# TensorE takes the turn and the routing of a step before the placing of the step ahead of it, in the third front of a transformer block

## The reference

```python
x = x + 0.5 * ffn(layernorm(x))          # 16 experts, two of them per token, and a shared expert
x = x + attention_and_moe(layernorm(x))  # linear attention, then 8 experts, two per token
x = x + 0.5 * ffn(layernorm(x))          # the first line again
```

```python
logits = jnp.einsum('btc,ec->bte', x, router_w)
top_vals, top_idx = jax.lax.top_k(logits, TOP_K)
gates = jax.nn.sigmoid(top_vals)
...
sg = jnp.einsum('btc,sc->bts', x, shared_gate_w)
su = jnp.einsum('btc,sc->bts', x, shared_up_w)
```

## Time and profile before

| | us |
|---|---|
| median of 3 runs | 840.58 (837.47 to 845.62) |
| the profiled execution | 843.14 |
| its span, first to last instruction | 841.4 |
| front3, from the first load of pairs to the first load of ffn3 | 539.17 to 664.22 |
| POOL busy over the span | 414.9 (49%) |
| PE busy over the span | 556.7 (66%) |
| granted TensorE clock, mean of the span | 0.808 |

### The profile page before, as it was taken

How to read it: one execution, slowest core, us unless ns; L and a number is a source line. 1 busy time by engine, 2 the same in 40 slices (tenths; PEclk the granted TensorE clock), 3 DMA queues, 4 the chain that set the end, 5 groups by cost and what they waited for, 6 DMA issues and landing times. The chain is left out here.

```text
span 841.4 us, 10790 instructions
## 1 busy us (share of the span) xinstructions
PE 556.7 (66%) x2860; PEld 414.7 (49%) x2860; DVE 385.1 (46%) x1192; ACT 282.3 (34%) x713; POOL 414.9 (49%) x444
## 2 busy tenths in 40 slices
PE   4897877883357879982396977337667187787720
PEld 3644766661235658761274755223223175676610
DVE  5781334331457669738311211278643044343327
ACT  5653333331143576631131313033434032232210
POOL 5217556544776551100466663247776045645540
PEclk9999899997567889965599897755767598989865
DMA  7151355441111110242111110242111222222228
GB/s 209 52 165 45 105 135 139 117 132 53 41 45 41 38 39 26 63 126 62 28 44 48 40 46 28 75 135 73 47 46 54 66 80 74 80 67 80 69 73 259
DMA packets 88518, 66.12 MB, mean 79 GB/s; under 512 B 10150, under 2 KB 80939, under 8 KB 88460
## 3 DMA queue, kind: packets, MB, share of 16 engines
q1 hardware_dynamic: 75596, 40.85, 17.1%
q0 software_dynamic: 11712, 24.04, 10.0%
q10 hardware_dynamic: 1152, 0.53, 0.2%
HBM read 36.63 MB, written 28.75 MB: 78 GB/s over the span
## 5 line engine op out<-in xcount | busy, mean ns | idle before, releaser
L1899 POOL DMA_INDIRECT ffn_pairs<-ffn_out,ffn_target x79 | 78.2, 990 | 81.1 <-ACT ffn_out L1980 42.5
L795 POOL DMA_INDIRECT ffn_rows<-norm_rows,core_gather_id x79 | 75.7, 958 | 58.7 <-issue 18.6
L299 POOL DMA_INDIRECT attn_back<-ffn_out_rows,core_back_slot x64 | 63.0, 984 | 34.3 <-issue 18.4
L1652 POOL DMA_INDIRECT expert_rows<-front_norm,front_slot_int x64 | 62.3, 973 | 27.9 <-issue 18.2
L1927 PE MATMUL ffn_gu_ps<-core_gate_up,ffn_rows_t 128*128 x158 | 50.4, 447 | 13.4 <-issue 8.3
L1481 POOL DMA_INDIRECT moe_pairs<-moe_out,core_scatter_id x40 | 39.4, 985 | 39.3 <-DVE moe_out L1566 29.5
L824 PE MATMUL ffn_gu_ps<-core_gate_up,ffn_rows_t 128*128 x158 | 46.2, 416 | 18.6 <-issue 11.1
L1542 ACT ACTIVATE moe_hid<-moe_hid_ps,core_b 128x320 f32<-128x320 f32 x64 | 31.7, 529 | 76.1 <-PE moe_hid_ps L1515 37.1
L893 DVE TENSOR_TENSOR ffn_hid<-ffn_gate,ffn_gu_ps 128x256 f32<-128x256 f32 (+1 forms) x40 | 16.7, 418 | 86.2 <-issue 63.2
L1992 DVE TENSOR_TENSOR ffn_hid<-ffn_gate,ffn_gu_ps 128x256 f32<-128x256 f32 (+1 forms) x40 | 16.7, 417 | 85.5 <-ACT ffn_gate L1973 50.3
L1515 PE MATMUL moe_hid_ps<-moe_rows_t,core_moe_w 128*128 128x320 f32 x128 | 42.5, 485 | 19.2 <-ACT moe_hid L1542 18.5
(11 more groups left out here) (275 smaller groups left out, 1353.7 us busy)
## 6 DMA issues: line engine op xcount, KB each, us to landing
ffn_rows<-expert_rows SPq DMA_DIRECT2D x79, 64.5 KB
ffn_out_rows<-ffn_out SPq DMA_DIRECT2D x39, 128.0 KB
core_moe_w<-in_w SPq DMA_DIRECT2D x8, 512.0 KB
moe_pairs<-core_zero SPq DMA_DIRECT2D x4, 1024.0 KB
front_pair<-moe_pairs SPq DMA_DIRECT2D x8, 512.0 KB, 5.0
last_pair<-ffn_pairs SPq DMA_DIRECT2D x8, 512.0 KB, 5.9
core_x<-in_x SPq DMA_DIRECT2D x8, 256.0 KB, 4.8
norm_rows<-front_norm SPq DMA_DIRECT2D x8, 256.0 KB, 2.2
```

Source lines behind the costliest of these rows:

```text
L299: pool.indirect_dma_start(out=self.got[j % self.depth][:, k, b, :], out_offset=None, in_=self.rows, in_offset=bass.IndirectOffsetOnAxis(ap ...
L795: pool.indirect_dma_start(out=rows[i % ring][:, h, :], out_offset=None, in_=core.norm_rows, in_offset=bass.IndirectOffsetOnAxis(ap=core.ga ...
L1652: pool.indirect_dma_start(out=core.expert_rows, out_offset=bass.IndirectOffsetOnAxis(ap=slot_int[:, j, g:g + 1], axis=0), in_=norm[j % rin ...
L1899: pool.indirect_dma_start(out=core.ffn_pairs, out_offset=bass.IndirectOffsetOnAxis(ap=target[:, n:n + 1], axis=0), in_=out[q % deep][:, h, ...
```

## The change

Only PE's loop in `front_scatter` is edited. `place` moves one turn of the loop down, with its argument lowered by one: in turn i PE now does the turn and the routing of step i, a unit, and then the placing of step i-1. The placing of step 7 falls into turn 8, between the units 12 and 13, and the totals follow in that turn too. No instruction is added or removed, and the queues of the other engines are the same row by row.

```diff
@@ -1831,11 +1831,11 @@
                 lo, hi = units_at(i)
                 if hi > lo:
                     units.product(nc, pe, core, lo, 0)
-                if i < S:
-                    place(i)
+                if 1 <= i <= S:
+                    place(i - 1)
                 for n in range(lo + 1, hi):
                     units.product(nc, pe, core, n, 0)
-                if i == S - 1:
+                if i == S:
                     pe.wait_ge(place_read, S)
```

## The result

The changed kernel took **869.98 us** (median of 4 runs, 863.90 to 872.23), the kernel before 841.04 (4 runs, 837.47 to 845.62). The ratio is 1.033, 95% interval 1.0255 to 1.0404: 3.3% slower, where 858.5 was forecast and 867 was the end of the range. The profiled execution took 872.23 us against 843.14, so 29.1 us are to be found. The mean granted clock is 0.805, against 0.808. Ratios leave out executions that count as disturbed by a slower state of the chip, on this one core by their time alone; none fell out here, but 6 of 12 did for the first kernel of experiment 5.

The account below looks back on a forecast made before the run. POOL was taken to set the pace at 11.54 us per step; a closed loop of 16.2 us per step, with start, table load and end, gave +17.9 us on the median of 840.58: 858.5 us, range 848 to 867.

Parts of the forecast that it names:

- case A: front3: the loop through POOL, ACT, PE and DVE closes with PE mostly slow, +13.7 to +21.1 us; chance 0.70.
- L: Chain from one step's first scatter to the next's in front3, taken as 16.2 us against POOL's 11.54 us.
- The walk: Sum of the chain's links in front3: 16.72 us per step with PE at 1.2 GHz, 13.99 at 2.4 GHz.
- table load: ACT's table load in step 3, between normalise and copy, now lies in the chain once: +1.28 us.
- End: End of front3: blanks 20.5 us behind placing 6, scatters last at 21.5, then 2.84 us to the next phase's load.
- bounds of 1 to 5 us: End of front3: bounds on the 2.84 us to the next load, as no row gave a scatter's landing time.
- Rival D: front3: late waits each count in the chain, or blanks or landing are slower; +27 to +30 us, chance 0.12.
- the one wait of POOL that the change was to remove: POOL's 3.87 us wait ahead of step 7 for slots, forecast to be gone in the new order.
- the upper bound of the gain: Earlier logits can only pay where POOL waits, ahead of step 7: at most 3.87 us.
- Rival C: front3: POOL stays the bound at 11.54 us per step, not slower; -2.6 us, 838, chance 0.06.
- The start: Start of front3: placing 0 waits for turn 1 and routing 1, at 559.30 in place of 558.05, +1.25 us.
- placing 7: Behind units 11 and 12, up to 7.04 us, covered by POOL's 9.80 us of scatters in step 6.

Follow-up runs that it names:

- experiment 5: Kernel before with blank tiles split SP 6, ACT 5, POOL 5: ratio 0.9984; first kernel, also with PE's placing ahead of the routing: ratio 0.9945.
- experiments 1: Changed kernel with the placing of step i-1 moved ahead of the shared expert's unit: 839.96 us, ratio 1.0073 to the kernel before.
- experiment 3: POOL's scaling of step j+2 moved behind all eight scatters of step j: changed kernel 889.43 us, ratio 1.0696; kernel before 833.43 us, ratio 1.0007.
- experiment 4: Changed kernel with POOL waiting for all 16 blank tiles ahead of step 7's scatters: 859.69 us in one run, 1.032 to the kernel before.
- experiment 2: Changed kernel with PE's order turn, placing of the preceding step, routing, unit, unit: 832.95 us, ratio 1.0022 to the kernel before.

## Why the prediction was right and where it failed

**Right: the loop and its price.** The mechanism of case A came out link by link, in the pace (experiments 1 and 3 move it by 3.6 and 5.2 us, where the links say 3.6 and 5.1), in the waits (the reader of the placing, L1754, waits 50.4 us in eight times, longest 8.9) and in what did not matter: the waits for logits in DVE's choice, up to 8.26 us in the earlier trace rows, are down to one of 2.1 us, and that bought nothing.

**Right in kind, short in size: L.** The walk gave 16.72 us with PE at 1.2 GHz and 13.99 at 2.4 GHz, and I took 16.2. The steps without the table load measured 16.58 to 16.76, since PE ran the head of every step at 1.2 GHz: the six together are +2.2 us over the forecast. (The walk itself was 0.14 us long, most of it in its first link, 6.34 for 6.15.) The 28% of fast clock that the earlier trace rows shows is there after too (0.65 over the six steps). But it falls behind the links of the chain: the unit behind the placing had a second product of 1.02 or 1.07 us in each step. All PE links of the chain stand ahead of that, right behind an idle stretch of 6.6 to 9.3 us in the steps 2 to 7, 7.12 in the rows shown. I had mixed a mean clock into a path on which only the slow part lies. The Trainium skill (TensorE: Matmul & The Clock Gate, section HAM oscillation — how this bites in real kernels) has the array cold again at each burst behind such a stretch; the trace agrees in each of these steps, with turns of 1.11 or 1.12 us and routings of 1.89, and the 16.72 that I set beside it was 0.14 off.

**Failed: the step "End".** There I let the blanks end 12.1 + 8.4 us behind placing 6, one microsecond ahead of the scatters, and gave the scatters 2.84 us to the next load. The 12.1 was right: 673.60 - 661.74 is 11.86. The 8.4 was wrong: beside scatters the eight issues took 16.74 us. In the kernel before ACT's blanks began at 653.00, after the last scatter's end at 652.36, so the earlier trace rows gave their price with POOL at rest. In the new order they begin 9.7 us ahead of that end. The tail became 10.60 us instead of 2.84, **+7.8 us**. That is the main miss. The sign that I passed over lay in the same trace, in the timeline of SP: its eight blanks, begun while POOL still scattered, took 11.34 us, though the last four of them, behind the last scatter, lie 1.09 us apart.

```profile
646.14 11.34 SPq L1626 DMA_DIRECT2D expert_rows<-front_blank  x8
```

The bounds of 1 to 5 us were set on the landing of a scatter, and experiment 4 puts that at 2.57; they were set on the wrong thing.

**Rival D.** It named the size (27 to 30 us) and, in its last sentence, blanks slower than I take them. But its main mechanism, late waits in the chain, did not occur: in the loop of the changed kernel ACT has no wait put down to "remote", where before it had five of 2.3 to 4.6 us, 16.2 together. In the tail came one such wait, DVE's of 8.85 us, beside ACT's slow issues. So that D's number fits is in part luck.

Those waits most likely explain the one wait of POOL that the change was to remove, too. ACT's timeline, kernel before, copies of the logits of steps 6 and 7:

```profile
623.21 0.22 ACT L1692 ACTIVATE front_logits<-front_logits_ps 128x64 f32<-128x64 f32 x1 [4.59 <-remote]
...
636.86 0.22 ACT L1692 ACTIVATE front_logits<-front_logits_ps 128x64 f32<-128x64 f32 x1 [3.18 <-remote]
```

The routings before them had ended at 620.04 and 634.28, so the copies came 3.2 and 2.6 us late, together more than 3.87. And in the profiled executions of experiment 3 (kernel before) and of experiment 5 (split alone) ACT has no such wait ahead of step 7, and that wait of POOL is absent. So the 3.87 us were a trait of some executions, and the upper bound of the gain was less firm than one row made it look.

**Rival C.** POOL's occupancy, the figure by which the Trainium skill (Perfetto Trace Analysis, section Identifying the Most-Contended Engine) picks what to work on, was 54.62 us of work before and 54.33 after in six steps; the time grew by 31 all the same. Experiment 3 says it more sharply.

**The rest.** The start was 1.53 for 1.25, the table load about 1.0 for 1.28, placing 7 was covered as said; 1.5 us of the profiled difference lie ahead of front3, where nothing was edited. From 17.9 the terms lead to 28.2: +7.8 for the tail, +2.2 for the pace, +0.3 for the start.

## What to carry to other kernels

When an instruction moves behind another on an engine that takes its work in order, walk once around every loop that this closes and compare its length with the busiest engine's step: up to that length the move is free (experiment 2), beyond it each microsecond counts once per step. On the loop use the durations of the place where each link will stand: here the matmuls behind PE's idle stretches of 6.6 to 9.3 us all cost their slow price, while the mean granted clock was 0.65. And before a transfer's or an issue's price is carried to a new place, look at what the other queues did while it was measured.

## What was not expected of the hardware

Beside POOL's indirect DMAs the queues of other engines can be held. Instructions with a median of 29 ns took up to 1409 ns, ACT's eight issues 15.5 to 16.7 us in place of 8.1 to 8.4, and ACT and DVE show waits of 2 to 9 us (once 13.8) whose releaser the trace calls "remote". In the stretches of this kind that were read, the DMA engines were busy for only 14 to 29% of the time.

Scatters under way seem to be needed: experiment 4 and the six prices beside it say so for the issues. They aren't enough. In the changed kernel's loop, where POOL rests 5.46 us in each step, ACT shows no such wait; but in experiments 2 and 3 (kernel before), where POOL scattered through all steps without waiting, its first also comes only in the tail, at 628.12 and 634.63. What decides between these stretches, and what inside the scatters does it (how they write their descriptors, a queue shared with the other issuers, the row writes themselves), no run here tells apart, and it stays open. That the blanks were left out altogether was not tried.
